# Attention with softmax sums by matmul: the sums lag one key chunk further behind, without an opening batch

## The chip, the cores and the metric

The kernel runs on all 8 cores of one Trainium2 chip. Each core does one half of one of four sequences and talks to no other core. The metric is the device time, in microseconds (us), of the slowest of the eight cores.

## The reference, cut to what matters

```python
def attn(x, Wq, Wk, Wv):                 # x: (4, 4096, 1024), 16 heads of 64
    q, k, v = (heads(x @ W.T) for W in (Wq, Wk, Wv))
    energy = einsum('nhqd,nhkd->nhqk', q, k)
    a = softmax(energy / sqrt(64), axis=3)
    return einsum('nhql,nhld->nhqd', a, v)

x = layernorm(x + attn(x, Wq, Wk, Wv))
x = layernorm(x + moe(x))                # 16 experts, the 6 best per token weighted, 1024x1024 each
```

The softmax is computed without a running maximum: the kernel takes exp(0.125 * energy - 3), sums the exponentials over the keys (the sums are called Z here), and divides the attention output by Z at the end.

## The kernel before, in words

A core holds keys and values of all 4096 tokens of its sequence and queries of its own 2048. It works in three stages: the projections K, V, Q (`proj_pass`), the attention, then the first layer norm with the router, the experts and the second layer norm (`p3_tile`, `ffn_unit`, `ln2_tile`). Each engine has its own list of work, written out in program order, and waits on semaphores. There is no scheduler: what stands first in the source stands first on the engine.

The attention is 16 passes over the keys, called pairs: 2 halves of 1024 queries (h) by 8 pairs of heads (c). A pair is 32 steps, kc = 0 to 31, one chunk of 128 keys each. In step kc TensorE (PE) is given, in this order:

- the scores S(kc): four matmuls of 512 queries, L352, two for each of the two heads. The scores of head 0 go to PSUM columns 0 to 1023, those of head 1 to 1024 to 2047. There is one such place per head, so the scores of a head wait until ScalarE (ACT) has taken the exponential of that head's scores of step kc-1 (semaphore sE, L349).
- in step 2 alone, `emit_ftz`: eight transposes (L313) of the Z of the pair before, which VectorE (DVE) then picks apart in sixteen small copies (L324, L326, the function `fvz`).
- PV(kc-1): four matmuls, L288, of the values with the exponentials of the step before, accumulated in PSUM columns 2048 to 3071.
- Z: four matmuls, L301, with a vector of ones instead of the values, accumulated in columns 3072 to 4095. These are the same columns that the transposes of step 2 use, so the first Z of a pair waits for `fvz`.

ACT is given in step kc two exponentials of 128 x 1024, L407 for head 0 and L410 for head 1, into one of four buffers, `pbuf(kc % 4)`. So the exponential of step kc (called exp kc below: its first half, L407) also waits until Z(kc-4), the last reader of that buffer, is done. That wait is on the semaphore tV, taken from the table `z_cnt` (L402 to L404).

Which Z stands in which step is set by the list `zl` (L382 to L386): none in steps 0 to 3, then Z(0), Z(1) and Z(2) as one batch of twelve matmuls in step 4, and Z(kc-2) from step 5 on. The batch has one semaphore increment, at its end. After step 31 follow PV(31) (`ftPVl`) and the two sums that are left, Z(30) and Z(31) (`ftZl`, L422). Then DVE moves both accumulators out of PSUM (L434, L436), and the next pair begins with S(0).

Of the kernel before, what the change touches and what calls it, by code (L numbers as in the profile page):

```python
# [19 lines left out]
NKT = 32  # L20
# [13 lines left out]
def build():  # L34
    NKT = SQ // 128
# [66 lines left out]
    def pbuf(par):  # L102
        return RC[:, par * 2048:(par + 1) * 2048]
# [57 lines left out]
    def q(eng, fn):  # L161
        SC[eng].append(fn)
# [119 lines left out]
    def emit_pv(t, c, kcp, first, last):  # L282
        P = pbuf(kcp % 4)
        for head in range(2):
            hh = 2 * c + head
            orow = slice(head * 64, (head + 1) * 64)
            for qc in range(2):
                ins = t.matmul(  # L288
                    PS[orow, 2048 + qc * 512: 2048 + (qc + 1) * 512],
                    RB[:, kcp * D + hh * 64: kcp * D + (hh + 1) * 64],  # L290
                    P[:, head * 1024 + qc * 512: head * 1024 + (qc + 1) * 512],
                    start=first, stop=last, tile_position=(0, head * 64),
                    skip_group_check=True)
        return ins

    def emit_z(t, c, kcp, first, last):
        P = pbuf(kcp % 4)
        for head in range(2):
            orow = slice(head * 64, (head + 1) * 64)
            for qc in range(2):  # L300
                ins = t.matmul(  # L301
                    PS[orow, 3072 + qc * 512: 3072 + (qc + 1) * 512],
                    ozb[:, :],
                    P[:, head * 1024 + qc * 512: head * 1024 + (qc + 1) * 512],
                    start=first, stop=last, tile_position=(0, head * 64),
                    skip_group_check=True)
        return ins

    def emit_ftz(p_prev):
        def ftz(t, zev=fve_cnt[p_prev]):  # L310
            t.wait_ge(vE, zev)
            for sl in range(8):
                ins = t.transpose(PS[:, 3072 + sl * 128: 3072 + (sl + 1) * 128],  # L313
                                  zs[:, sl * 128:(sl + 1) * 128], idf[:, :])
            ins.then_inc(tV, 1)
        q("tensor", ftz)
        ctV.v += 1
        ztr = ctV.v

        def fvz(v, c=p_prev % NPAIR, h=p_prev // NPAIR, ztr=ztr):  # L320
            v.wait_ge(tV, ztr)
            for sl in range(8):
                tile = h * 8 + sl
                v.tensor_copy(rzpre[:, tile * NH + 2 * c: tile * NH + 2 * c + 1],  # L324
                              PS[:, 3072 + sl * 128: 3072 + sl * 128 + 1])
                ins = v.tensor_copy(  # L326
                    rzpre[:, tile * NH + 2 * c + 1: tile * NH + 2 * c + 2],
                    PS[:, 3072 + sl * 128 + 64: 3072 + sl * 128 + 65])
            ins.then_inc(vE, 1)
        q("vector", fvz)  # L330
        cvE.v += 1
        fvz_cnt[p_prev] = cvE.v

    for h in range(2):
        for c in range(NPAIR):
            p = h * NPAIR + c
            qc0 = h * 1024

            for kc in range(NKT):
                exp_need = csE.v  # L340
                first_pair_wait = p1_ve if (p == 0 and kc == 0) else 0

                def ftS(t, c=c, kc=kc, qc0=qc0, exp_need=exp_need,
                        fw=first_pair_wait):
                    if fw > 0:
                        t.wait_ge(vE, fw)
                        t.wait_ge(gC, consts_done)
                    for head in range(2):
                        t.wait_ge(sE, max(0, exp_need - 1 + head))  # L349
                        rows = slice(head * 64, (head + 1) * 64)  # L350
                        for qc in range(2):
                            ins = t.matmul(  # L352
                                PS[:, head * 1024 + qc * 512:
                                   head * 1024 + (qc + 1) * 512],
                                RA[rows, c * SQ + kc * 128: c * SQ + (kc + 1) * 128],
                                QO[rows, c * TOK + qc0 + qc * 512:
                                   c * TOK + qc0 + (qc + 1) * 512],
                                start=True, stop=True, tile_position=(head * 64, 0))
                        if head == 0:
                            ins.then_inc(tS, 1)  # L360
                    ins.then_inc(tS, 1)
                q("tensor", ftS)
                ctS.v += 2
                s_done = ctS.v

                if kc == 2 and p > 0:
                    emit_ftz(p - 1)

                if kc > 0:
                    kcp = kc - 1  # L370
                    ve_need = fve_cnt.get(p - 1, 0) if kcp == 0 else 0

                    def ftPV(t, c=c, kcp=kcp, exp_need=exp_need, ve_need=ve_need):
                        t.wait_ge(sE, exp_need)
                        if ve_need > 0:
                            t.wait_ge(vE, ve_need)
                        emit_pv(t, c, kcp, kcp == 0, False).then_inc(tV, 1)
                    q("tensor", ftPV)
                    ctV.v += 1
                    pv_cnt[(p, kcp)] = ctV.v  # L380

                zl = []  # L382
                if kc == 4:
                    zl = [0, 1, 2]
                elif kc >= 5:
                    zl = [kc - 2]  # L386
                if zl:
                    ve_need = fvz_cnt.get(p - 1, 0) if zl[0] == 0 else 0

                    def ftZ(t, c=c, zl=tuple(zl), ve_need=ve_need):  # L390
                        if ve_need > 0:
                            t.wait_ge(vE, ve_need)
                        for kcp in zl:
                            ins = emit_z(t, c, kcp, kcp == 0, False)
                        ins.then_inc(tV, 1)
                    q("tensor", ftZ)
                    ctV.v += 1
                    for kcp in zl:
                        z_cnt[(p, kcp)] = ctV.v

                def fse(sc, s_done=s_done, kc=kc,
                        pv_need=(z_cnt.get((p, kc - 4), 0) if kc >= 4 else 0)):  # L402
                    if pv_need > 0:
                        sc.wait_ge(tV, pv_need)  # L404
                    P = pbuf(kc % 4)
                    sc.wait_ge(tS, s_done - 1)
                    sc.activation(P[:, 0:1024], PS[:, 0:1024], AF.Exp,  # L407
                                  bias=cb3[:, :], scale=0.125).then_inc(sE, 1)
                    sc.wait_ge(tS, s_done)
                    sc.activation(P[:, 1024:2048], PS[:, 1024:2048], AF.Exp,  # L410
                                  bias=cb3[:, :], scale=0.125).then_inc(sE, 1)
                q("scalar", fse)
                csE.v += 2

            def ftPVl(t, c=c, exp_need=csE.v):
                t.wait_ge(sE, exp_need)
                emit_pv(t, c, NKT - 1, False, True).then_inc(tV, 1)
            q("tensor", ftPVl)
            ctV.v += 1
            pv_cnt[(p, NKT - 1)] = ctV.v  # L420

            def ftZl(t, c=c):  # L422
                for kcp in (NKT - 2, NKT - 1):
                    ins = emit_z(t, c, kcp, False, kcp == NKT - 1)
                ins.then_inc(tV, 1)
            q("tensor", ftZl)
            ctV.v += 1
            for kcp in (NKT - 2, NKT - 1):
                z_cnt[(p, kcp)] = ctV.v
            pvz_done = ctV.v  # L430

            def fve(v, c=c, qc0=qc0, pvz_done=pvz_done):
                v.wait_ge(tV, pvz_done)
                v.tensor_copy(QO[:, c * TOK + qc0: c * TOK + qc0 + 1024],  # L434
                              PS[:, 2048:3072])
                ins = v.tensor_copy(zs[:, :], PS[:, 3072:4096])  # L436
                ins.then_inc(vE, 1)
            q("vector", fve)
            cvE.v += 1
            fve_cnt[p] = cvE.v  # L440
# [426 lines left out]
```

## Time and profile before

| | us |
|---|---|
| median of two runs | 3036.62 |
| the two runs | 2975.59 and 3097.65 |
| the profiled execution | 2974.15 |
| span of its slowest core, core 4 | 2972.6 |
| spans of its eight cores | 2951.4 to 2972.6 |

The profile is of one execution, and its rows are of core 4 where no other core is named. The span runs from the first instruction of the program on a core to the last; 1.55 us of the execution's time lie outside it. The attention stands on core 4 between about 344 and 1645 us of the span. Rows of a timeline show instructions of one engine in order of time, with the idle time of the engine in front of them in brackets and who ended it. In such a row, matmuls on PE overlap each other, so the time from one row's start to the next row's start says more than a row's length.

### The profile page before, as it was taken

What the parts mean: (1) busy time and instruction counts of PE and PEld (TensorE: products, weight loads), DVE (VectorE), ACT (ScalarE), POOL (GpSimd) and SP (SyncE); (2) the same over time, 40 slices, a digit from 0 to 9 for tenths busy, and PEclk for the clock granted to TensorE, in tenths of its full rate; (3) what the DMA queues carried; (4) which work ended last, traced back from release to release, by engine and by line L of the source; (5) the groups of instructions that cost most, each with busy time, mean ns of one, the idle gap of its engine ahead of it and who ended that gap; (6) DMA issues with size and microseconds to landing.
All of it is one profiled execution on the core that took longest, in us unless ns stands there. A gap on an engine that the chain in (4) does not pass through costs nothing.

```text
span 2972.6 us, 31977 instructions; the slowest of 8 cores (2951.4 to 2972.6 us)
## 1 busy us (share of the span) xinstructions
PE 2388.8 (80%) x12032; PEld 908.2 (31%) x12032; DVE 718.8 (24%) x1555; ACT 1119.0 (38%) x1153; POOL 59.8 (2%) x80
## 2 busy tenths in 40 slices
PE   5996989888888888888889333799996343799996
PEld 2443322222222222222222111344442121344442
DVE  2332200000000000000000434233336434233336
ACT  0000288888888888888888010000000101000000
POOL 1000100000000000000000000000000000000000
PEclk9998899999999999999998667899998666899998
DMA  6645899930000000000000200221223100221221
GB/s 87 99 72 85 99 107 110 111 57 1 1 1 1 1 1 1 1 1 1 1 1 1 85 22 7 85 77 65 85 84 107 43 14 7 85 85 57 85 85 57
DMA packets 48017, 146.90 MB, mean 49 GB/s; under 512 B 2752, under 2 KB 23264, under 8 KB 46848
## 3 DMA queue, kind: packets, MB, share of 16 engines
q0 software_dynamic: 43264, 128.09, 23.2%
q1 hardware_dynamic: 4608, 16.78, 1.6%
q8 instruction: 103, 1.69, 0.3%
q14 instruction: 42, 0.34, 0.0%
HBM read 197.32 MB, written 41.94 MB: 80 GB/s over the span
## 4 chain that ended last, share of the span: by engine, by line
PE 68%; ACT 13%; DVE 8%; issue 7%; DMA 3%; DVEq 1%; ACTq 0%; POOL 0%; SPq 0%; POOLq 0%
PE s_PS L686 30%; PE s_PS L352 13%; ACT s_RC L410 10%; PE s_PS L288 9%; PE s_PS L225 5%; PE s_PS L301 5%; PE s_PS L246 4%; DVE s_RC L509 2%; DMA s_RC<-xfm 1%; ACT s_RC L407 1%; PE s_PS L313 1%; DMA s_RC<-xqf 1%; DVE s_RA L700 1%; DMA s_RB<-ewb 1%; DVE s_RC L516 1%
## 5 line engine op out<-in xcount | busy, mean ns | idle before, releaser
L686 PE MATMUL s_PS<-s_RB,s_QO 128*128 128x512 bf16 x4096 | 931.6, 391 | 132.8 <-DVE s_gates L642 67.3
L352 PE MATMUL s_PS<-s_QO,s_RA 64*128 64x512 bf16 x2048 | 589.6, 399 | 145.3 <-ACT s_RC L410 82.2
L407 ACT ACTIVATE s_RC<-s_PS,s_cb 128x1024 bf16<-128x1024 f32 x512 | 570.6, 1115 | 221.8 <-PE s_PS L352 157.5
L686 PEld LDWEIGHTS s_PS<-s_RB,s_QO 128*128 128x128 bf16 x4096 | 407.3, 100 | 653.2 <-issue 203.5
L410 ACT ACTIVATE s_RC<-s_PS,s_cb 128x1024 bf16<-128x1024 f32 x512 | 567.3, 1108 | 2.5 <-PE s_PS L352 2.3
L288 PE MATMUL s_PS<-s_RC,s_RB 128*64 128x512 bf16 x2048 | 344.2, 416 | 11.7 <-ACT s_RC L410 11.7
L744 ACT ACTIVATE s_tE<-s_tB 128x1 f32<-128x1 f32 x16 | 3.2, 203 | 876.1 <-DVE s_tB L736 876.1
L301 PE MATMUL s_PS<-s_RC,s_ozb 128*64 128x512 bf16 x2048 | 320.6, 402 | 0.0
L434 DVE CAST s_QO<-s_PS 128x1024 bf16<-128x1024 f32 x16 | 19.6, 1224 | 1157.3 <-PE s_PS L301 1157.3
L352 PEld LDWEIGHTS s_PS<-s_QO,s_RA 64*128 64x128 bf16 x2048 | 118.4, 94 | 582.0 <-issue 581.5
L703 DVE SCALAR_TENSOR_TENSOR s_RB<-s_PS,s_gates,s_RA 128x1024 f32<-128x1024 f32 x128 | 164.2, 1283 | 275.4 <-PE s_PS L686 275.4
L225 PE MATMUL s_PS<-s_RC 128*128 128x512 bf16 x768 | 170.8, 386 | 57.4 <-DMA s_RC<-xfm 33.4
L706 DVE SCALAR_TENSOR_TENSOR s_RA<-s_PS,s_gates,s_RB 128x1024 f32<-128x1024 f32 x112 | 143.8, 1284 | 267.2 <-PE s_PS L686 267.2
L563 PE MATMUL s_PS<-s_idb,s_RC 128*128 128x128 bf16 x128 | 16.2, 305 | 189.9 <-ACT s_RC L555 189.9
L301 PEld LDWEIGHTS s_PS<-s_RC,s_ozb 128*64 128x64 bf16 x2048 | 127.1, 116 | 111.3 <-issue 19.3
L288 PEld LDWEIGHTS s_PS<-s_RC,s_RB 128*64 128x64 bf16 x2048 | 76.5, 111 | 243.3 <-issue 243.3
L537 ACT ACTIVATE s_tE<-s_tB 128x1 f32<-128x1 f32 x16 | 3.2, 203 | 347.0 <-DVE s_tB L528 347.0
L407 ACT ACT_TABLE_LOAD x1 | 1.3, 1283 | 344.9 <-PE s_PS L352 344.9
L225 PEld LDWEIGHTS s_PS<-s_RC 128*128 128x128 bf16 x768 | 75.9, 99 | 151.9 <-issue 64.8
L246 PE MATMUL s_PS<-s_QO,s_RC 128*128 128x512 bf16 x512 | 111.9, 382 | 2.9 <-DMA s_RC<-xfm 2.9
L662 POOL DMA_DIRECT2D s_RB<-ewb x32 | 28.3, 885 | 2534.2 <-PE s_PS L313 1317.3
L563 PEld LDWEIGHTS s_PS<-s_idb,s_RC 128*128 128x128 bf16 x128 | 12.4, 137 | 196.8 <-issue 196.8
(76 smaller groups left out, 645.4 us busy)
## 6 DMA issues: line engine op xcount, KB each, us to landing
s_RB<-ewb POOLq DMA_DIRECT2D x32, 2048.0 KB, 9.6
ewb<-ew POOLq DMA_DIRECT2D x16, 2048.0 KB, 172.0
s_RC<-xfm POOLq DMA_DIRECT2D x16, 1024.0 KB, 10.0
s_RC<-xtm SPq DMA_DIRECT2D x16, 512.0 KB, 3.5
y<-s_RC SPq DMA_DIRECT2D x16, 512.0 KB, 2.6
s_RC<-xqf POOLq DMA_DIRECT2D x4, 1024.0 KB, 17.7
s_RC<-wkT POOLq DMA_DIRECT2D x1, 2048.0 KB, 18.5
s_QO<-wvT POOLq DMA_DIRECT2D x1, 2048.0 KB, 26.7
```

The source lines that it names most:

```text
L225: ins = t.matmul(bank(b), wtile[:, dc * 1024 + jc * 128: dc * 1024 + (jc + 1) * 128], xstage(par)[:, dc * 512:(dc + 1) * 512], start=(dc = ...
L246: ins = t.matmul(bank(b), xstage(par)[:, dc * 512 + tt * 128: dc * 512 + (tt + 1) * 128], wtile[:, dc * 1024 + jh * 512: dc * 1024 + (jh + ...
L288: ins = t.matmul(PS[orow, 2048 + qc * 512: 2048 + (qc + 1) * 512], RB[:, kcp * D + hh * 64: kcp * D + (hh + 1) * 64], P[:, head * 1024 + q ...
L301: ins = t.matmul(PS[orow, 3072 + qc * 512: 3072 + (qc + 1) * 512], ozb[:, :], P[:, head * 1024 + qc * 512: head * 1024 + (qc + 1) * 512], ...
L313: ins = t.transpose(PS[:, 3072 + sl * 128: 3072 + (sl + 1) * 128], zs[:, sl * 128:(sl + 1) * 128], idf[:, :])
L352: ins = t.matmul(PS[:, head * 1024 + qc * 512: head * 1024 + (qc + 1) * 512], RA[rows, c * SQ + kc * 128: c * SQ + (kc + 1) * 128], QO[row ...
L407: sc.activation(P[:, 0:1024], PS[:, 0:1024], AF.Exp, bias=cb3[:, :], scale=0.125).then_inc(sE, 1)
L410: sc.activation(P[:, 1024:2048], PS[:, 1024:2048], AF.Exp, bias=cb3[:, :], scale=0.125).then_inc(sE, 1)
L509: v.scalar_tensor_tensor(u_f32[:, sg * 64:(sg + 1) * 64], PS[:, pcol + sg * 64: pcol + (sg + 1) * 64], rz[:, t_i * NH + sg: t_i * NH + sg ...
L686: ins = t.matmul(PS[:, pb + jh * 512: pb + (jh + 1) * 512], QO[:, dc * TOK + t_i * 128: dc * TOK + (t_i + 1) * 128], wbuf(par)[:, dc * 102 ...
L703: v.scalar_tensor_tensor(accB(tt), PS[:, pb: pb + 1024], g, accA(tt), ALU.mult, ALU.add).then_inc(vE, 1)
L706: v.scalar_tensor_tensor(accA(tt), PS[:, pb: pb + 1024], g, accB(tt), ALU.mult, ALU.add).then_inc(vE, 1)
```

## The change

`zl` no longer has a batch. Z(kc-3) stands in each step from step 3 on: Z(0) in step 3, Z(1) in step 4, and so on to Z(28) in step 31. Three sums instead of two are left for `ftZl` at the end of the pair. The table `z_cnt` follows: exp kc still waits for Z(kc-4), which now stands in step kc-1 instead of step kc-2, and for exp 4 in step 3 instead of in the batch of step 4. The wait for `fvz`, which belongs to Z(0), moves with it from step 4 to step 3.

```diff
-                if kc == 4:
-                    zl = [0, 1, 2]
-                elif kc >= 5:
-                    zl = [kc - 2]
+                if kc >= 3:
+                    zl = [kc - 3]
                 if zl:
                     ve_need = fvz_cnt.get(p - 1, 0) if zl[0] == 0 else 0
...
             def ftZl(t, c=c):
-                for kcp in (NKT - 2, NKT - 1):
+                for kcp in (NKT - 3, NKT - 2, NKT - 1):
                     ins = emit_z(t, c, kcp, False, kcp == NKT - 1)
                 ins.then_inc(tV, 1)
             q("tensor", ftZl)
             ctV.v += 1
-            for kcp in (NKT - 2, NKT - 1):
+            for kcp in (NKT - 3, NKT - 2, NKT - 1):
                 z_cnt[(p, kcp)] = ctV.v
```

On PE, from S(3) of the second pair on, there stood before (S is L352, PV is L288, Z is L301):

```order
L352 MATMUL s_PS<-s_QO,s_RA 128x512 x4
L288 MATMUL s_PS<-s_RC,s_RB 64x512 x4
L352 MATMUL s_PS<-s_QO,s_RA 128x512 x4
L288 MATMUL s_PS<-s_RC,s_RB 64x512 x4
L301 MATMUL s_PS<-s_RC,s_ozb 64x512 x12
L352 MATMUL s_PS<-s_QO,s_RA 128x512 x4
L288 MATMUL s_PS<-s_RC,s_RB 64x512 x4
L301 MATMUL s_PS<-s_RC,s_ozb 64x512 x4
```

In the changed kernel the same place, from S(3) on, reads:

```order
L352 MATMUL s_PS<-s_QO,s_RA 128x512 x4
L288 MATMUL s_PS<-s_RC,s_RB 64x512 x4
L301 MATMUL s_PS<-s_RC,s_ozb 64x512 x4
L352 MATMUL s_PS<-s_QO,s_RA 128x512 x4
L288 MATMUL s_PS<-s_RC,s_RB 64x512 x4
L301 MATMUL s_PS<-s_RC,s_ozb 64x512 x4
L352 MATMUL s_PS<-s_QO,s_RA 128x512 x4
L288 MATMUL s_PS<-s_RC,s_RB 64x512 x4
```

The twelve Z matmuls behind PV(3) have become four; four have moved up into step 3, and from there on each step carries four.

At the end of the first pair, from S(31) to S(0) and S(1) of the second, PE had before:

```order
L352 MATMUL s_PS<-s_QO,s_RA 128x512 x4
L288 MATMUL s_PS<-s_RC,s_RB 64x512 x4
L301 MATMUL s_PS<-s_RC,s_ozb 64x512 x4
L288 MATMUL s_PS<-s_RC,s_RB 64x512 x4
L301 MATMUL s_PS<-s_RC,s_ozb 64x512 x8
L352 MATMUL s_PS<-s_QO,s_RA 128x512 x8
```

And in the changed kernel:

```order
L352 MATMUL s_PS<-s_QO,s_RA 128x512 x4
L288 MATMUL s_PS<-s_RC,s_RB 64x512 x4
L301 MATMUL s_PS<-s_RC,s_ozb 64x512 x4
L288 MATMUL s_PS<-s_RC,s_RB 64x512 x4
L301 MATMUL s_PS<-s_RC,s_ozb 64x512 x12
L352 MATMUL s_PS<-s_QO,s_RA 128x512 x8
```

The last run of Z matmuls, which the next pair's S(0) stands behind, has grown from eight to twelve. The number of matmuls of a pair is the same.

## Rows read from the trace of the kernel before

**Rows 1.** The page, part 1: busy time and share of the span by engine.
```profile
PE 2388.8 (80%) x12032; PEld 908.2 (31%) x12032; DVE 718.8 (24%) x1555; ACT 1119.0 (38%) x1153; POOL 59.8 (2%) x80
```

**Rows 2.** Span and mean granted TensorE clock of core 1.
```profile
core 1: 2970.3 us, clock 0.904
```

**Rows 3.** Waits of ACT on core 4: us in total, times, longest us.
```profile
ACT s_RC L407 <- PE s_PS L301: 60.3, 16, 4.9
```

**Rows 4.** Timeline of ACT, third pair, exp 3, exp 4 and exp 7: start, us.
```profile
514.96 1.11 ACT L407 ACTIVATE s_RC<-s_PS,s_cb 128x1024 bf16<-128x1024 f32 x1 [1.93 <-PE s_PS L352]
...
521.40 1.11 ACT L407 ACTIVATE s_RC<-s_PS,s_cb 128x1024 bf16<-128x1024 f32 x1 [4.32 <-PE s_PS L301]
...
529.04 1.11 ACT L407 ACTIVATE s_RC<-s_PS,s_cb 128x1024 bf16<-128x1024 f32 x1 [0.28 <-PE s_PS L352]
```

**Rows 5.** Timeline of ACT, fifth pair, exp 3, exp 4, exp 5 and exp 7.
```profile
678.26 1.11 ACT L407 ACTIVATE s_RC<-s_PS,s_cb 128x1024 bf16<-128x1024 f32 x1 [2.15 <-PE s_PS L352]
...
683.13 1.11 ACT L407 ACTIVATE s_RC<-s_PS,s_cb 128x1024 bf16<-128x1024 f32 x1 [2.75 <-PE s_PS L301]
...
685.14 1.11 ACT L407 ACTIVATE s_RC<-s_PS,s_cb 128x1024 bf16<-128x1024 f32 x1
...
689.61 1.11 ACT L407 ACTIVATE s_RC<-s_PS,s_cb 128x1024 bf16<-128x1024 f32 x1
```

**Rows 6.** Timeline of ACT, second pair, exp 7 and exp 31.
```profile
445.32 1.11 ACT L407 ACTIVATE s_RC<-s_PS,s_cb 128x1024 bf16<-128x1024 f32 x1
...
498.98 1.11 ACT L407 ACTIVATE s_RC<-s_PS,s_cb 128x1024 bf16<-128x1024 f32 x1
```

**Rows 7.** Timeline of PE, end of the second pair, then steps 3, 4 and 7 of the third.
```profile
503.89 1.06 PE L301 MATMUL s_PS<-s_RC,s_ozb 128*64 128x512 bf16 x8
504.89 0.61 PE L352 MATMUL s_PS<-s_QO,s_RA 64*128 64x512 bf16 x4
...
514.80 0.63 PE L288 MATMUL s_PS<-s_RC,s_RB 128*64 128x512 bf16 x4
516.22 0.59 PE L352 MATMUL s_PS<-s_QO,s_RA 64*128 64x512 bf16 x2 [0.80 <-ACT s_RC L407]
...
518.46 2.78 PE L301 MATMUL s_PS<-s_RC,s_ozb 128*64 128x512 bf16 x12
522.65 0.59 PE L352 MATMUL s_PS<-s_QO,s_RA 64*128 64x512 bf16 x2 [1.41 <-ACT s_RC L407]
...
529.89 0.60 PE L301 MATMUL s_PS<-s_RC,s_ozb 128*64 128x512 bf16 x4
530.42 0.60 PE L352 MATMUL s_PS<-s_QO,s_RA 64*128 64x512 bf16 x2
```

**Rows 8.** Windows, third pair: PE, PEld, DVE, ACT, POOL busy (count), then granted clock, DMA.
```profile
507.70:514.50 6.80, 6.65 (x26) 2.47 (x26) 1.14 (x16) 4.25 (x5) 0.00 (x0) 0.50 0.85 95
514.50:517.90 3.40, 2.19 (x14) 0.54 (x12) 0.00 (x0) 2.12 (x2) 0.00 (x0) 1.00 1.11 125
517.90:521.30 3.40, 3.34 (x16) 1.14 (x12) 0.00 (x0) 0.00 (x0) 0.00 (x0) 0.50 1.37 145
...
524.70:528.10 3.40, 3.40 (x18) 0.86 (x14) 0.00 (x0) 2.28 (x3) 0.00 (x0) 0.51 1.09 116
528.20:589.60 61.40, 55.02 (x320) 16.32 (x318) 2.35 (x2) 55.07 (x54) 0.00 (x0) 1.00 1.01 112
```

**Rows 9.** Timeline of DVE, third pair: the last of the sixteen copies of fvz.
```profile
514.22 0.15 DVE L326 COPY s_rzpre<-s_PS 128x1 f32<-128x1 f32 x1
```

**Rows 10.** Waits of ACT on core 1: us in total, times, longest us.
```profile
ACT s_RC L407 <- PE s_PS L301: 52.9, 16, 4.9
```

**Rows 11.** Windows, a part of the last pair (columns as in rows 8).
```profile
1558.90:1579.40 20.50, 18.50 (x68) 5.41 (x68) 1.14 (x16) 10.70 (x11) 0.00 (x0) 0.50 0.00 1
```

**Rows 12.** Timeline of ACT, last pair, exp 4 and exp 7.
```profile
1571.09 1.11 ACT L407 ACTIVATE s_RC<-s_PS,s_cb 128x1024 bf16<-128x1024 f32 x1 [4.87 <-PE s_PS L301]
...
1579.89 1.11 ACT L407 ACTIVATE s_RC<-s_PS,s_cb 128x1024 bf16<-128x1024 f32 x1 [0.50 <-PE s_PS L352]
```

## The prediction

> **What bounds the kernel now.** I read the page first. PE is busy for 80% of the span and ACT for 38% [rows 1], which makes PE look like the bound. But the change touches only the attention, so I asked the timelines how one step of it is paced. In the even part of a pair, from exp 7 to exp 31, 24 steps take 53.66 us, or 2.236 us each [rows 6]. ACT alone can do a step in less: in the fifth pair exp 5 follows exp 4 by 2.01 us, with no idle time in front of it [rows 5]. So even the even part is paced by a ring in which exponentials and matmuls release each other, a little longer than ACT's own work. Moving matmuls matters only where it makes that ring longer or shorter.
>
> The view of the waits then shows one line that belongs to the batch: ACT's first exponential waits for a Z matmul (L301) 16 times, once per pair, 60.3 us in total [rows 3]. The timeline shows where. In the third pair exp 4 starts 6.44 us after exp 3, and 4.32 us of that ACT sits idle until the batch of twelve Z matmuls ends [rows 4]. PE pays as well: its next scores, S(5), wait 1.41 us for exp 4 [rows 7]. In the fifth pair the same gap is 4.87 us, 2.75 us of it idle [rows 5]. What differs is the clock: in the third pair the batch ran at a granted clock of 0.50, the lower of TensorE's two levels, 1.2 GHz [rows 8].
>
> **The change, part by part.**
>
> *The wait of exp 4.* It now needs Z(0) alone, which stands in step 3. After PV(2) of step 3 PE idles 0.80 us before S(4) [rows 7], because S(4) waits for exp 3. Four Z matmuls take 0.53 us from start to start [rows 7], so Z(0) fits in that idle time and S(4) starts when it did. Exp 4 then finds its scores and its buffer ready and follows exp 3 at ACT's own pace of 2.01 us [rows 5]. What comes next is late in its turn: from exp 4 on, each step carries PV and Z, so I take the four steps from exp 3 to exp 7 at the even pace, 4 x 2.236 = 8.94 us. Before, they took 14.08 us in the third pair [rows 4] and 11.35 us in the fifth [rows 5]. The first difference is 5.14, which is the wait of 4.32 and 0.82 more; the second is 2.41, the wait of 2.75 less 0.34, because PE now has a Z to do in steps that were free of one. Of core 4's sixteen pairs, twelve are like the third and four like the fifth. The total is 60.3 + 12 x 0.82 - 4 x 0.34 = 68.8 us gained.
>
> *The clock inside that.* The 0.82 contains a claim. In the third pair the clock fell to 0.50 three times: for 6.8 us near the pair's start, then twice for 3.4 us [rows 8]. Before the second fall PE was busy only 2.19 of 3.40 us [rows 8], in which its waits for exp 3 lie. Z(0) fills 0.53 us of exactly that stretch, and the long wait before S(5) goes with the batch. In the even part, with short waits in every step, the clock stays at 1.00 [rows 8]. So I expect the second and third fall to go, and the first to stay, since nothing before step 3 changes.
>
> *The end of the pair.* Twelve instead of eight Z matmuls stand before the next S(0), and ACT has nothing to do there. Eight take 1.00 us from start to start, four take 0.53 [rows 7]; four more cost 0.47. Times 16 this is 7.5 us lost, all on the path. The copies of the accumulators on DVE, the transposes and S(0) all move back by the same amount, so nothing else comes late there.
>
> *Waits that are moved.* Z(0)'s wait for fvz now stands one step earlier, and S(4) and everything behind it on PE would wait too. The last copy of fvz starts at 514.22 and takes 0.15 us; PV(2) starts at 514.80 [rows 7, 9]. The wait is met 0.4 us before PV(2) even starts, so it costs 0. Exp kc's wait for Z(kc-4) moves one step later, but S(kc), which exp kc needs anyway, stands behind that Z on PE. The wait can never end last, so it costs 0 and cannot gain.
>
> *Z(0) at the low clock.* In some pairs the first fall still lasts when step 3 is reached. At half the clock Z(0) takes about twice 0.53, or 1.06 us, an estimate, against 0.80 us of idle time [rows 7]. That makes S(4) 0 to 0.3 us late, 0 to 4.8 us over sixteen pairs. I take 2.5.
>
> *Sum on core 4:* 68.8 - 7.5 - 2.5 = 58.8 us. *On the slowest core:* core 1 ends at 2970.3 [rows 2], 2.3 us before core 4's 2972.6, but its wait for Z is only 52.9 us [rows 10], 7.4 less. Its gain is 58.8 - 7.4 = 51.4, so it ends at 2970.3 - 51.4 = 2918.9, behind core 4 at 2972.6 - 58.8 = 2913.8. With the 1.55 us outside the span the forecast is 2920.5 us, against the profiled execution's 2974.15: 1.8% less. That execution agrees with the faster of the two runs, 2975.59; the median of 3036.62 also holds the slower one, and the forecast is meant for an execution like the profiled one.
>
> **The rivals.**
>
> *The falls of the clock stay where they are.* Short waits at the pair's start remain: those for exp 0 to exp 3 are untouched. If these alone cause the later falls, every pair gains what the fifth does, 2.41 - 0.47 = 1.94 us, 31 us in all, and the time is 2943. For it: the third pair's last fall begins at 524.7, nearly 10 us after exp 3 [rows 4, 8], well behind the place of Z(0). Against it: the falls follow waits that the change removes. A rule stands on this side: the Trainium skill (TensorE: Matmul & The Clock Gate, "A second HAM failure mode: psum-queue depth-cycling") says that frequent small idle times between groups of matmuls make the clock swing, and the change turns one dense batch into small groups. By that rule the even part, with a wait in every step, would swing as well; the trace shows 1.00 there for 61.40 us [rows 8], and so the rule gets a minor chance.
>
> *PE is the bound after all.* If its 80% [rows 1] were real work, moving matmuls would gain nothing: 2974. The idle times in front of S(4) and S(5) [rows 7] speak against it, and that ACT waited 60.3 us for the batch.
>
> *Slower: the clock stays low deep into the pair.* The batch is a dense run of matmuls, and it may be what brings the clock back. Once it is spread out, the low level could last. In the last pair it held for 20.5 us [rows 11], with steps from exp 4 to exp 7 of (1579.89 - 1571.09) / 3 = 2.93 us [rows 12], 0.70 more than the even pace. It decides from 51.4 / 16 / 0.70 = 4.6 added steps at the low clock per pair; ten such steps cost 112 us, and the time is 2974 - 51 + 112 = 3035. Against it: in the third pair the clock was back at 514.5, before any Z [rows 8]; and that 20.5 us stretch contained the batch, which did not end it.
>
> *More than forecast.* If core 1 gains what core 4 does without the low-clock loss, and the first fall also ends earlier in some pairs, another 20 to 25 us go: 2897.
>
> **How the numbers follow.** The forecast gets 0.69, the falls that stay 0.15, PE as the bound 0.05, the slower case 0.04, more than forecast 0.07. The forecast's own spread is 2900 to 2935: 2.5 us for the term at the low clock, 8 for which core is last, 8 for how the falls happen to lie. The bound of 2%, about what a measurement of this kernel can tell from no change, is 2914.7, inside that spread, with about half of the forecast's chance below it. Faster by over 2%: 0.35 + 0.07 = 0.42. Within 2%: 0.34 + 0.15 + 0.05 = 0.54. Slower: 0.04. The range runs from 2897, the better case, to 2958, past the falls that stay; outside lie PE as the bound, the slower case and half of the better case, some 0.13.
>
> **What would show it.** Right, step by step: the wait of L407 for L301 is gone from the view of ACT's waits; exp 4 follows exp 3 by about 2.0 us; the four steps from exp 3 take near 9 us in nearly all pairs; the low clock appears once per pair; the time from exp 31 to the next exp 0 grows by 0.4 to 0.5 us; the even pace stays at 2.236. Wrong: falls after step 4 in most pairs, a wait of L301 for L326 in step 3, a new even pace, or a first fall that lasts beyond exp 4.

## The result and the profile after

| | before | after |
|---|---|---|
| median, us | 2980.06 (10 runs) | 2917.59 (11 runs) |
| ratio of the times | 1 | 0.9787, 95% interval 0.9759 to 0.9815 |
| profiled execution, us | 2974.15 | 2914.67 |
| its slowest core's span, us | 2972.6 | 2913.1 |

A run on all eight cores is sometimes some per cent longer whatever the kernel; the medians hold such runs, the ratio leaves them out. The changed kernel is 2.1% faster. The interval reaches across 2% on both sides.

The waits of ACT (ScalarE) on core 4, which is the slowest core here too. L405 is the line that was L407, the first exponential of a step:

```profile
ACT s_RC L405 <- PE s_PS L352: 141.2, 224, 2.7
```

The line of [rows 3] has no successor: in 16 pairs ACT waits for no Z matmul (L301) any more, where it waited 60.3 us.

The timeline of ACT, third pair: exp 3, exp 4, exp 7, exp 31 and the fourth pair's exp 0 (start, length, idle before):

```profile
509.10 1.11 ACT L405 ACTIVATE s_RC<-s_PS,s_cb 128x1024 bf16<-128x1024 f32 x1 [2.50 <-PE s_PS L352]
...
511.11 1.11 ACT L405 ACTIVATE s_RC<-s_PS,s_cb 128x1024 bf16<-128x1024 f32 x1
...
518.05 1.11 ACT L405 ACTIVATE s_RC<-s_PS,s_cb 128x1024 bf16<-128x1024 f32 x1 [0.34 <-PE s_PS L352]
...
572.00 1.11 ACT L405 ACTIVATE s_RC<-s_PS,s_cb 128x1024 bf16<-128x1024 f32 x1 [0.34 <-PE s_PS L352]
...
576.82 1.11 ACT L405 ACTIVATE s_RC<-s_PS,s_cb 128x1024 bf16<-128x1024 f32 x1 [2.70 <-PE s_PS L352]
```

Exp 4 follows exp 3 by 2.01 us, where [rows 4] had 6.44 and [rows 5] 4.87. The four steps from exp 3 to exp 7 take 8.95 us instead of 14.08. From exp 7 on the pace is what it was: 53.95 us for 24 steps, the same as in the third pair before (the pair of [rows 6], with 53.66 us, is the second, and takes that after the change too). The end of the pair, from exp 31 to the next exp 0, takes 4.82 us.

The timeline of PE (TensorE), third pair, PV(2), Z(0) and S(4), and then the end of that pair:

```profile
508.94 1.04 PE L288 MATMUL s_PS<-s_RC,s_RB 128*64 128x512 bf16 x4
509.80 0.62 PE L301 MATMUL s_PS<-s_RC,s_ozb 128*64 128x512 bf16 x4
510.36 0.59 PE L352 MATMUL s_PS<-s_QO,s_RA 64*128 64x512 bf16 x2
...
574.69 1.49 PE L301 MATMUL s_PS<-s_RC,s_ozb 128*64 128x512 bf16 x12
576.12 0.61 PE L352 MATMUL s_PS<-s_QO,s_RA 64*128 64x512 bf16 x4
```

In [rows 7] PE idled 0.80 us between PV(2) and S(4). Now Z(0) stands there, and no wait is marked in front of S(4). Twelve Z matmuls at the end take 1.43 us from start to start, where eight took 1.00.

The granted clock in the same pair (windows view; columns as in [rows 8], the granted clock is the third figure from the end):

```profile
503.00:509.80 6.80, 6.80 (x29) 2.53 (x27) 1.14 (x16) 3.81 (x4) 0.00 (x0) 0.50 0.74 82
509.90:579.90 70.00, 62.13 (x370) 18.75 (x366) 2.35 (x2) 62.22 (x62) 0.00 (x0) 1.00 1.01 110
```

One stretch at the low level is left, near the start; the two later ones of [rows 8] are gone. On core 4 that holds in all sixteen pairs, and no pair of any other core has a later fall either: in the 128 pairs of the eight cores, a fall began between exp 3 and exp 4 in 48 before and in none after, and behind exp 4 in 93 before and in none after. Two cores' spans, for the step of the sum that went wrong:

```profile
core 1: 2897.9 us, clock 0.915
...
core 4: 2913.1 us, clock 0.913
```

### The profile page after: what moved, and what is told of

The parts are those of the page before. It is cut to its first block, busy times and chain, and to the rows that moved or that the text cites. A ratio compares the mean times of both kernels' runs of the same rounds, so it can differ in the third digit from the quotient of the medians.

```text
span 2913.1 us, 31977 instructions; the slowest of 8 cores (2897.9 to 2913.1 us)
## 1 busy us (share of the span) xinstructions
PE 2361.5 (81%) x12032; PEld 903.0 (31%) x12032; DVE 718.7 (25%) x1555; ACT 1122.9 (39%) x1153; POOL 59.7 (2%) x80
## 4 chain that ended last, share of the span: by engine, by line
PE 62%; ACT 16%; issue 9%; DVE 8%; DMA 4%; DVEq 1%; ACTq 0%; POOL 0%; SPq 0%; POOLq 0%
PE s_PS L684 30%; PE s_PS L352 11%; ACT s_RC L408 10%; PE s_PS L288 6%; PE s_PS L225 5%; PE s_PS L301 4%; ACT s_RC L405 4%; PE s_PS L246 4%; DVE s_RC L507 2%; DMA s_RC<-xfm 1%; PE s_PS L313 1%; DMA s_RC<-xqf 1%; DMA s_RB<-ewb 1%; DVE s_RA L698 1%; DVE s_RC L514 1%
## 5 line engine op out<-in xcount | busy, mean ns | idle before, releaser
L352 PE MATMUL s_PS<-s_QO,s_RA 64*128 64x512 bf16 x2048 | 590.8, 390 | 107.1 <-ACT s_RC L408 69.5
L405 ACT ACTIVATE s_RC<-s_PS,s_cb 128x1024 bf16<-128x1024 f32 x512 | 570.6, 1114 | 152.4 <-PE s_PS L352 141.2
L288 PE MATMUL s_PS<-s_RC,s_RB 128*64 128x512 bf16 x2048 | 334.5, 406 | 12.8 <-ACT s_RC L408 12.8
L301 PE MATMUL s_PS<-s_RC,s_ozb 128*64 128x512 bf16 x2048 | 306.0, 382 | 0.0
L352 PEld LDWEIGHTS s_PS<-s_QO,s_RA 64*128 64x128 bf16 x2048 | 117.9, 94 | 539.7 <-issue 539.7
L301 PEld LDWEIGHTS s_PS<-s_RC,s_ozb 128*64 128x64 bf16 x2048 | 123.2, 111 | 101.6 <-issue 4.4
L288 PEld LDWEIGHTS s_PS<-s_RC,s_RB 128*64 128x64 bf16 x2048 | 75.6, 110 | 236.6 <-issue 236.6
## 6 DMA issues: line engine op xcount, KB each, us to landing
s_RB<-ewb POOLq DMA_DIRECT2D x32, 2048.0 KB, 10.2
```

The costliest lines, as they stand in the source:

```text
L288: ins = t.matmul(PS[orow, 2048 + qc * 512: 2048 + (qc + 1) * 512], RB[:, kcp * D + hh * 64: kcp * D + (hh + 1) * 64], P[:, head * 1024 + q ...
L301: ins = t.matmul(PS[orow, 3072 + qc * 512: 3072 + (qc + 1) * 512], ozb[:, :], P[:, head * 1024 + qc * 512: head * 1024 + (qc + 1) * 512], ...
L352: ins = t.matmul(PS[:, head * 1024 + qc * 512: head * 1024 + (qc + 1) * 512], RA[rows, c * SQ + kc * 128: c * SQ + (kc + 1) * 128], QO[row ...
L405: sc.activation(P[:, 0:1024], PS[:, 0:1024], AF.Exp, bias=cb3[:, :], scale=0.125).then_inc(sE, 1)
```

## The experiments

The runs ask four things: which part of the change brings the gain, what the clock falls from, whether its even spread of Z is needed, and whether its cost at the end of the pair can be had back. The theory is that of the prediction. In all timelines below the first exponential of a step stands for the step. Expectations call TensorE's falls to its low level "falls". The first, second and third fall of a pair are those of [rows 8]: the first begins before exp 3, the second between exp 3 and exp 4, the third behind exp 4. Averages over eight cores are of all 128 pairs of a run's profiled execution.

**One signal for each Z of the batch.** An edit of the kernel before:

```diff
                         for kcp in zl:
                             ins = emit_z(t, c, kcp, kcp == 0, False)
-                        ins.then_inc(tV, 1)
+                            ins.then_inc(tV, 1)
                     q("tensor", ftZ)
-                    ctV.v += 1
                     for kcp in zl:
+                        ctV.v += 1
                         z_cnt[(p, kcp)] = ctV.v
```

> Before, but each Z of the batch in step 4 signals by itself, so exp 4 waits for Z(0) and no longer for Z(1) and Z(2) behind it. Theory (the place of Z(0), behind PV(3), is most of the loss; the common signal of twelve matmuls is the rest): exp 4 follows exp 3 by about 4.0 us where it was 4.87 and by about 4.7 where the clock is low, and the time falls by 13 to 27 us, to 2947 to 2961. Rival (the common signal is all of it): exp 4 follows exp 3 by 2.0 us and the time is that of the changed kernel, 2918.

Measured: 2926.61 us, ratio to before 0.9825 (0.9767 to 0.9882). Its slowest core, ACT's wait for Z:

```profile
ACT s_RC L407 <- PE s_PS L301: 37.3, 16, 3.1
```

Its timeline of ACT, third pair, exp 3, exp 4 and exp 7:

```profile
509.62 1.11 ACT L407 ACTIVATE s_RC<-s_PS,s_cb 128x1024 bf16<-128x1024 f32 x1 [2.75 <-PE s_PS L352]
...
513.62 1.11 ACT L407 ACTIVATE s_RC<-s_PS,s_cb 128x1024 bf16<-128x1024 f32 x1 [1.88 <-PE s_PS L301]
...
520.10 1.11 ACT L407 ACTIVATE s_RC<-s_PS,s_cb 128x1024 bf16<-128x1024 f32 x1
```

And its timeline of PE, the batch and S(5):

```profile
512.86 1.47 PE L301 MATMUL s_PS<-s_RC,s_ozb 128*64 128x512 bf16 x12
514.88 0.59 PE L352 MATMUL s_PS<-s_QO,s_RA 64*128 64x512 bf16 x2 [0.56 <-ACT s_RC L407]
```

Exp 4 came 4.00 us after exp 3, as the theory said, so the rival (2.0 us) is wrong. But the time fell by some 47 us, from 2973.96 for the kernel before beside it, where the theory allowed 13 to 27. The expectation counted only exp 4 itself. PE's wait before S(5) also shrank, from 1.41 us [rows 7] to 0.56, and with it went the third fall of the clock in every pair of this core, and of the other seven; the second is left in eight pairs of this core, and in 67 of the 128 pairs of all cores. Averaged over the pairs of core 7, exp 3 to exp 7 fell from 13.28 to 11.06 us, 36 us in all. Another 15 us came from exp 0 to exp 3, which fell from 9.21 to 8.30 us, with a first fall that was shorter or absent in more pairs; no theory had foreseen that, and no run shows how the edit does it. On the average of the eight cores exp 3 to exp 7 took 13.19 us before, 11.13 here and 9.05 in the changed kernel. So of what the change takes out of these four steps about half hung on the signal that came only after twelve matmuls, and the other half on the place of Z(0).

**The half of the change that moves Z(0).** An edit of the kernel before:

```diff
-                if kc == 4:
-                    zl = [0, 1, 2]
+                if kc == 3:
+                    zl = [0]
+                elif kc == 4:
+                    zl = [1, 2]
                 elif kc >= 5:
                     zl = [kc - 2]
```

> Half of the change: Z(0) moves to step 3, Z(1) and Z(2) stay as a batch of eight matmuls in step 4, the lag stays at two steps and the end of the pair at eight Z matmuls. Theory (only Z(0)'s place matters; four more matmuls cost 0.42 to 0.47 us wherever the ring carries them): exp 3 to exp 7 takes 9.4 us instead of 8.94, exp 31 to the next exp 0 takes 4.38 instead of 4.82, and the time is within 5 us of the changed kernel's 2918. Rival (the even spread itself is what keeps the clock up): falls of the clock behind step 4 in half of the pairs or more, and 2930 or above.

Measured: 2913.66 us, ratio 0.9783 (0.9709 to 0.9857); the changed kernel's 0.9787 lies within the interval. The timeline of ACT on core 4: exp 31 of the second pair, then exp 0, exp 3 and exp 7 of the third:

```profile
490.24 1.11 ACT L409 ACTIVATE s_RC<-s_PS,s_cb 128x1024 bf16<-128x1024 f32 x1 [0.34 <-PE s_PS L352]
494.62 1.11 ACT L409 ACTIVATE s_RC<-s_PS,s_cb 128x1024 bf16<-128x1024 f32 x1 [2.27 <-PE s_PS L352]
...
503.86 1.11 ACT L409 ACTIVATE s_RC<-s_PS,s_cb 128x1024 bf16<-128x1024 f32 x1 [2.44 <-PE s_PS L352]
...
513.23 1.11 ACT L409 ACTIVATE s_RC<-s_PS,s_cb 128x1024 bf16<-128x1024 f32 x1 [0.34 <-PE s_PS L352]
```

The end of the pair takes 4.38 us and exp 3 to exp 7 takes 9.37, both as the theory said, and no pair of any core has a second or third fall. The even spread is not what brings the gain: four matmuls taken from the end of the pair and given to step 4 cost there what they saved.

**Two sums in the idle time of step 3.** An edit of the kernel before:

```diff
-                if kc == 4:
-                    zl = [0, 1, 2]
-                elif kc >= 5:
+                if kc == 3:
+                    zl = [0, 1]
+                elif kc >= 4:
                     zl = [kc - 2]
```

> Z(0) and Z(1) both in step 3, then Z(kc-2), so the end of the pair has eight Z matmuls as before the change. Theory (PE's idle time before S(4), 0.80 us, and the slack behind it hide eight Z matmuls of 0.95 us): exp 3 to exp 7 stays near 8.94 us, exp 31 to the next exp 0 takes 4.38, and the time is 5 to 7 us below the changed kernel's 2918. Rival (in pairs whose first low-clock stretch reaches step 3 the eight matmuls take twice as long and S(4) comes late): exp 3 to exp 4 rises above 2.6 us in half of the pairs, and the time is 2917 to 2922.

Measured: 2907.99 us, ratio 0.9767 (0.9719 to 0.9815). That is 7 us below the changed kernel in its second measurement (2915.13, next but one), though the intervals of the ratios overlap, and 10 us below the 2918 of the expectation. Both theories had a part in it. In ten pairs of the slowest core exp 4 follows exp 3 by 2.01 us and exp 7 comes after 8.95. In four it comes after 2.65 to 2.72 us, as in the sixth pair, of which these are exp 3 and exp 4 (the first two pairs differ, as they do in the changed kernel):

```profile
735.40 1.12 ACT L407 ACTIVATE s_RC<-s_PS,s_cb 128x1024 bf16<-128x1024 f32 x1 [2.74 <-PE s_PS L352]
...
738.11 1.12 ACT L407 ACTIVATE s_RC<-s_PS,s_cb 128x1024 bf16<-128x1024 f32 x1 [0.59 <-PE s_PS L352]
```

Most of those 0.7 us is caught up by exp 7, which comes after 9.14 to 9.21 us in these four. The average of all sixteen pairs from exp 3 to exp 7 is 9.14 us against 9.06 in the changed kernel, while the end of the pair, at 4.39 us, is 0.43 us shorter.

**More work, and faster.** The kernel before, with four matmuls added whose result is thrown away:

```diff
+                if kc == 3:
+                    def ftZx(t, c=c, ve_need=fvz_cnt.get(p - 1, 0)):
+                        if ve_need > 0:
+                            t.wait_ge(vE, ve_need)
+                        emit_z(t, c, 0, True, False)
+                    q("tensor", ftZx)
                 zl = []
                 if kc == 4:
                     zl = [0, 1, 2]
```

> Before, with Z(0) computed once more in step 3, four matmuls whose result the batch of step 4 overwrites; the wait for the batch stays. It fills PE's idle time before S(4) and does nothing else. Theory (the second fall of the clock follows that idle time): the second fall is gone in nearly all pairs, the batch runs at the full clock, the wait of exp 4 falls from 4.3 to 2.75 us in the pairs that had the fall, exp 3 to exp 7 lies between 11.35 and 12.9 us, and the time falls by 16 to 33 us, to 2941 to 2958. Rival (the falls come from the waits of steps 0 to 2, which are still there): the second fall stays and the time is 2974 to 2980.

Measured: 2952.86 us, ratio 0.9913 (0.9882 to 0.9943). The waits of ACT on its slowest core, core 1 (the core had 52.9 before, [rows 10]):

```profile
ACT s_RC L414 <- PE s_PS L301: 45.3, 16, 4.1
```

Its timeline of ACT, third pair, exp 3, exp 4 and exp 7:

```profile
509.65 1.11 ACT L414 ACTIVATE s_RC<-s_PS,s_cb 128x1024 bf16<-128x1024 f32 x1 [0.92 <-PE s_PS L352]
...
514.51 1.11 ACT L414 ACTIVATE s_RC<-s_PS,s_cb 128x1024 bf16<-128x1024 f32 x1 [2.75 <-PE s_PS L301]
...
522.21 1.11 ACT L414 ACTIVATE s_RC<-s_PS,s_cb 128x1024 bf16<-128x1024 f32 x1 [0.42 <-PE s_PS L352]
```

On PE, Z(0) with the thrown-away result, S(4), the batch and S(5):

```profile
509.94 0.60 PE L301 MATMUL s_PS<-s_RC,s_ozb 128*64 128x512 bf16 x4
510.90 0.59 PE L352 MATMUL s_PS<-s_QO,s_RA 64*128 64x512 bf16 x2 [0.36 <-ACT s_RC L414]
...
512.88 1.47 PE L301 MATMUL s_PS<-s_RC,s_ozb 128*64 128x512 bf16 x12
515.77 0.59 PE L352 MATMUL s_PS<-s_QO,s_RA 64*128 64x512 bf16 x2 [1.42 <-ACT s_RC L414]
```

And the windows of that pair:

```profile
509.00:514.00 5.00, 4.22 (x34) 1.54 (x32) 0.70 (x11) 2.12 (x2) 0.00 (x0) 1.00 0.97 105
514.50:517.90 3.40, 1.72 (x10) 0.63 (x12) 0.00 (x0) 3.39 (x4) 0.00 (x0) 1.00 1.39 159
517.90:521.40 3.50, 3.50 (x18) 0.81 (x12) 0.00 (x0) 2.48 (x3) 0.00 (x0) 0.51 0.98 112
```

The batch now runs at the full clock, and exp 4 follows exp 3 by 4.86 or 4.87 us in fifteen of the sixteen pairs, where core 1 had over 5 us in six pairs before. Over all eight cores a fall began between exp 3 and exp 4 in 48 of 128 pairs before and begins there in none here, though the wait for the batch is still there: the second fall did follow PE's idle time before S(4). The third fall is still there in eight pairs, this one among them (60 pairs of all cores, 93 before); before it PE was busy only 1.72 of 3.40 us and waited for exp 4. By the ratios this run gives 0.9% of the change's 2.1%. On the average of the eight cores the attention became 24 us shorter: 17 us in the four steps from exp 3 to exp 7, the rest before exp 3, where the first fall was absent in more pairs.

**The changed kernel once more,** beside the next runs.

> The changed kernel itself once more, beside the next two. Both theories: 2914 to 2921, and in at least 14 of 16 pairs exp 3 to exp 7 takes 8.9 to 9.0 us.

Measured: 2915.13 us, ratio 0.9793 (0.9774 to 0.9812); on the slowest core fourteen of sixteen pairs take 8.94 or 8.95 us from exp 3 to exp 7, and the first two 10.30 and 9.22.

**The lag lengthened once more.** An edit of the changed kernel (with four sums in `ftZl`):

```diff
-                if kc >= 3:
-                    zl = [kc - 3]
+                if kc >= 4:
+                    zl = [kc - 4]
```

> The lag doubled once more against the change: Z(kc-4) in step kc, from step 4 on, four sums left for the end. Exp kc then waits for a Z that stands behind its own scores and behind PV(kc-1). Theory (the change's longer lag is free only because Z(kc-4) stands ahead of S(kc) on PE): the ring now holds scores, PV, Z and both exponentials one after another, 0.14 + 0.52 + 0.46 + 0.6 + 0.1 + 2.12 = 3.9 us a step instead of 2.24, 28 steps in 16 pairs, some 760 us: near 3680, and up to 4300 if the idle time on PE brings the low clock. Rival (four buffers give room enough for one more step): 2910 to 2935.

Measured: 4304.76 us, one run. The waits of ACT, 28 in each of 16 pairs:

```profile
ACT s_RC L405 <- PE s_PS L301: 1411.5, 448, 3.5
```

Two steps of its even part, on ACT:

```profile
705.43 1.12 ACT L405 ACTIVATE s_RC<-s_PS,s_cb 128x1024 bf16<-128x1024 f32 x1 [3.16 <-PE s_PS L301]
...
710.72 1.12 ACT L405 ACTIVATE s_RC<-s_PS,s_cb 128x1024 bf16<-128x1024 f32 x1 [3.16 <-PE s_PS L301]
```

On PE, S, PV and Z of one of them:

```profile
706.70 2.01 PE L352 MATMUL s_PS<-s_QO,s_RA 64*128 64x512 bf16 x4 [1.42 <-ACT s_RC L405]
708.64 1.07 PE L288 MATMUL s_PS<-s_RC,s_RB 128*64 128x512 bf16 x4
709.49 1.07 PE L301 MATMUL s_PS<-s_RC,s_ozb 128*64 128x512 bf16 x4
```

And the windows view there:

```profile
700.00:780.00 80.00, 57.95 (x180) 12.28 (x180) 0.00 (x0) 32.37 (x31) 0.00 (x0) 0.50 0.00 0
```

A step takes 5.29 us. The ring holds the matmuls and the exponentials one after another, PE idles 1.42 us in each step, and the clock is at 0.50 for the 80 us shown: the upper end of what the theory said. That it is the idle time which holds the clock down fits the run above, but no run took it away at this lag. The change stands one step away from this: its longer lag is free only because Z(kc-4) stands ahead of S(kc).

**The next pair's scores ahead of the last sums.** An edit of the changed kernel: S(0) of the next pair (`ftSn`, the same matmuls as in `ftS`) is given to PE before PV(31), and step 0 of pairs 2 to 16 issues its exponentials alone.

```diff
+            if p < 2 * NPAIR - 1:
+                def ftSn(t, c=(p + 1) % NPAIR, qc0=((p + 1) // NPAIR) * 1024,
+                         exp_need=csE.v):
...
+                q("tensor", ftSn)
+                ctS.v += 2
             def ftPVl(t, c=c, exp_need=csE.v):
```

> The changed kernel, with the next pair's S(0) ahead of PV(31) and the twelve last Z matmuls, so that ACT has exp 0 to do beside them. Theory (the end of the pair is on the path because S(0) stands behind the sums): exp 31 to the next exp 0 falls from 4.82 to 2.0 us; PV(0) then waits for DVE's copies and gives 1 to 2 us back; the net is 0.7 to 2 us in each of 15 pairs, more where the first fall of the clock goes with the idle time, so 2875 to 2907. Rival (the wait of PV(0) for DVE's copies takes its place in full): 2912 to 2922.

Measured: 2885.95 us, ratio 0.9700 (0.9681 to 0.9719). The timeline of ACT on its slowest core, exp 31 of the second pair, exp 0 (L347 here) and exp 1 of the third:

```profile
491.99 1.11 ACT L418 ACTIVATE s_RC<-s_PS,s_cb 128x1024 bf16<-128x1024 f32 x1 [0.34 <-PE s_PS L365]
...
494.00 1.11 ACT L347 ACTIVATE s_RC<-s_PS,s_cb 128x1024 bf16<-128x1024 f32 x1
...
497.33 1.11 ACT L418 ACTIVATE s_RC<-s_PS,s_cb 128x1024 bf16<-128x1024 f32 x1 [1.21 <-PE s_PS L365]
```

The waits of PE: PV(0) for DVE's (VectorE's) second copy:

```profile
PE s_PS L288 <- DVE s_RC L467: 31.4, 15, 2.4
```

Exp 0 follows exp 31 by 2.01 us instead of 4.82. Part comes back: exp 1 follows exp 0 by 3.33 instead of 2.01, and PV(0) waits some 2 us for the copies, a wait that was not there before. From exp 0 to exp 3 a pair of this core takes 9.97 us on average, against 8.94 on the same core in the second measurement of the changed kernel, so some 1.8 of the 2.8 us stay. The rival named the wait rightly but not its weight. The first fall became shorter, as the theory had allowed: on this core it lasts 3.4 us in fourteen of the sixteen pairs, and 6.8 us in eleven in that measurement.

**Both savings together,** the order of the run before with the lists of the third experiment.

> S(0) ahead of PV(31) as in the run before, with Z(0) and Z(1) in step 3 and Z(kc-2) after, so eight sums' matmuls at the end of the pair instead of twelve. Theory (both savings are on the path and add up): 5 to 10 us below the run before. Rival (the end of the pair is now hidden behind exp 0, and its length counts no more): within 3 us of the run before.

Measured: 2877.07 us, ratio 0.9668 (0.9649 to 0.9687), 9 us below the run before. On ACT of its slowest core, exp 31, exp 0 and exp 1 (L420 here):

```profile
493.01 1.11 ACT L420 ACTIVATE s_RC<-s_PS,s_cb 128x1024 bf16<-128x1024 f32 x1 [0.34 <-PE s_PS L365]
...
495.02 1.11 ACT L347 ACTIVATE s_RC<-s_PS,s_cb 128x1024 bf16<-128x1024 f32 x1
...
497.91 1.11 ACT L420 ACTIVATE s_RC<-s_PS,s_cb 128x1024 bf16<-128x1024 f32 x1 [0.77 <-PE s_PS L365]
```

Exp 1 now follows exp 0 by 2.89 us: with eight instead of twelve Z matmuls ahead of it, S(1) comes 0.44 us earlier. The savings add up, and this version beats both kernels.

## Why the prediction was right

The forecast was 2920.5 us for an execution like the profiled one of before; the profiled one of after took 2914.67, and the median after is 2917.59. Core 4's span fell by 59.5 us where its sum said 58.8. Step by step:

- *The wait of exp 4* went in full, and exp 3 to exp 4 became 2.01 us in nine of core 4's pairs, 2.25 to 2.33 in six and 3.81 in the first. The four steps to exp 7 were priced at 8.94; they take 8.94 in fourteen of core 4's sixteen pairs, 10.51 in the first and 9.22 in the second, 9.06 on average. Before, they averaged 13.41. The gain is 16 x (13.41 - 9.06) = 70 us, where the steps on the wait and on Z(0) at the low clock said 68.8 - 2.5 = 66.3. The steps were read at two pairs, and the sorting of the others by them was rough: of the twelve that were counted as like the third, pairs 7 and 15 had exp 4 after 4.87 us and took 12.9 us to exp 7, while the first and the last took 14.66 and 15.79.
- *The clock.* The second and third fall went and the first stayed, as said. The run with thrown-away matmuls shows the second to have followed the idle time before S(4), and the run with a signal of its own for each Z shows the third to go when the wait before S(5) shrinks. That wait does not bring a fall each time: in the fifth pair before, PE waited 1.42 us in front of S(5), and no fall followed. The rival that the falls stay did not come true: the spread-out sums ran at 1.00 for 70 us. The rule of the Trainium skill that was weighed beside it (TensorE: Matmul & The Clock Gate, "A second HAM failure mode: psum-queue depth-cycling"), that frequent small idle times between groups of matmuls make the clock swing, is not borne out by that row, in which PE still idles 0.35 us in front of a head's scores. In the run with the longest lag, with an idle time of 1.42 us on PE in every step, the clock was low but did not swing: it stayed at 0.50 for the 80 us shown.
- *Z(0) at the low clock* does make S(4) late, as in pairs with exp 4 at 2.3 instead of 2.0 us, but the next step made up for it. Except in the first two pairs it cost nothing by exp 7; these two are 1.85 us above 8.94 together, against the 2.5 us of the term. In the first pair of core 4 the fall lasted 10.2 us, past exp 4, which the prediction had named as a sign of being wrong; it is the only such pair of this core.
- *The end of the pair* costs 4.82 - 4.38 = 0.44 us a pair, against 0.47.
- *The moved waits* cost nothing: no wait of L301 for L326 appears, and L301 ends no wait of ACT. The run with the longest lag shows where that ends: there L301 ends 28 waits of ACT in each pair.
- *Which core is last* was wrong. The sum took core 1, with a gain of 51.4 us. Core 1's span fell by 72.4 us, and core 4 remained the slowest. The step took the total of one wait for the gain. Core 1 waited 7.4 us less for Z than core 4, but in that same execution its exp 3 to exp 7 took 13.33 us on average, against 13.41 on core 4: most of what it saved in the wait it spent behind it. From the first exponential to the last, its attention became 59.5 us shorter. The rest of the 72.4 us is outside the attention, which began 8.6 us earlier on this core and had 4.2 us less behind it.

The step on the last core set the forecast 5.1 us higher than core 4's own sum, 2918.9 instead of 2913.8. With the 0.7 us by which core 4 beat its sum, these are the 5.8 us between the forecast and the profiled execution. That core 4's sum came out so close is in part luck. From the first exponential to the last, the attention became 64.7 us shorter there, 5.9 more than the sum. Its span shows 59.5 because it began the attention 0.7 us later and took 4.5 us longer for what follows, 1343.25 instead of 1338.76 us, which the change does not touch.

One thing the prediction did not say is how the gain divides between the place of Z(0) and the signal. The theory of the first experiment put most of the loss down to the place. The run shows that about half of what the four steps from exp 3 lost hung on the common signal: exp 4 needed one sum and waited for three, and giving each its own signal took 47 us off the time without moving an instruction.

## What to carry to other kernels

Where a buffer is released by a batch, ask which part of the batch the waiting engine needs, and signal that part by itself: with the signals alone the time fell by 1.75% (0.9825), with the work moved by 2.1% (0.9787). A stall of a microsecond on TensorE (0.80 us before S(4), 1.41 before S(5)) can be paid a second time in the granted clock of the work behind it, so a stall is priced by comparing pairs with and without the fall and not by its own length. Work moved to the end of a loop pass is on the path of the next pass. Putting the next pass's first instructions ahead of it took 29 us off here, but even then four Z matmuls fewer at the end were worth another 9.

## What was not expected of the hardware

Four matmuls more per pair, with a result that nobody reads, made the kernel 0.87% faster (0.9913, 0.9882 to 0.9943), because PE no longer fell to its low clock behind an idle time of 0.8 us, in any of 128 pairs. In the run with the longest lag the clock stayed at 0.50 although PE was busy 57.95 of 80.00 us. And pairs of the same instructions on the same core differ in their first fall: in the changed kernel's second measurement, on its slowest core and after the first pair, it lasted 3.4 us in some pairs, 6.8 in others, and was absent in one. What decides that was not tried; it goes with an exp 0 to exp 3 of between 7.1 and 9.5 us in those pairs, and in the run with a signal for each Z it gave 15 us on core 7 that no sum had foreseen.
